# A mixture-of-experts layer on one core: expert slots in 32 places of 256 columns instead of 16 of 512

## The reference

```
x = x + layernorm(attention(layernorm(x)))      # 16 heads, one shared k/v head, causal
x = x + layernorm(moe(layernorm(x)))
moe(x):  probs = softmax(x @ router.T); two best of 8 experts, weights renormalised
         expert e:  silu(x @ gate_e.T) * (x @ up_e.T) @ down_e.T      # 352 inner columns
         plus sigmoid(x @ shared_gate.T) * shared(x)                  # 1408 inner columns
```

## Time and profile before

| | us |
|---|---|
| median of three executions | 2177.38 |
| the profiled execution | 2180.47 |
| its span, first to last instruction | 2178.7 |
| attention | 0 to about 803 |
| routing and the first gathers | 803 to 877 |
| experts, first gate matmul to end of last down | 877.10 to 1424.24 |
| shared expert | 1429.46 to the end |

### The profile page before, as it was taken

The page is one execution under the profiler, slowest core; times in us unless marked ns, Lnnn a source line. Parts: engine busy times, 40 slices in busy tenths (PEclk is TensorE's granted clock), DMA queues, the critical chain, the costliest instruction groups (busy, mean ns, idle before and its releaser), DMA issues. The chain is left out here.

```text
span 2178.7 us, 30973 instructions
## 1 busy us (share of the span) xinstructions
PE 1989.7 (91%) x10858; PEld 1520.2 (70%) x10858; DVE 1037.5 (48%) x2158; ACT 700.6 (32%) x1350; POOL 468.4 (22%) x1045
## 2 busy tenths in 40 slices
PE   4989999999998723999999999999999999999995
PEld 3665656656666413777788888878888788888884
DVE  4556766666665328444445555443432424334243
ACT  3445545454454210344444444332111111111111
POOL 1223424233333221111111111001112021120212
PEclk9799999999998855999999999999999999999998
DMA  5134353343532213344445545332023020230202
GB/s 174 54 106 129 112 181 116 123 143 113 184 108 95 97 77 130 127 156 156 156 143 197 202 145 203 146 122 83 20 97 116 21 97 20 97 116 20 97 20 97
DMA packets 107019, 250.36 MB, mean 115 GB/s; under 512 B 10753, under 2 KB 25345, under 8 KB 99617
## 3 DMA queue, kind: packets, MB, share of 16 engines
q1 hardware_dynamic: 95392, 211.14, 28.4%
q0 software_dynamic: 11520, 37.76, 5.5%
HBM read 165.76 MB, written 79.69 MB: 113 GB/s over the span
## 5 line engine op out<-in xcount | busy, mean ns | idle before, releaser
L1251 PE MATMUL ex_bank<-ex_xT,ex_gu 128*128 128x512 f32 (+14 forms) x1656 | 346.8, 368 | 5.4 <-DVE ex_xT L1285 5.4
L1251 PEld LDWEIGHTS ex_bank<-ex_xT,ex_gu 128*128 128x128 f32 (+1 forms) x1656 | 277.9, 183 | 70.4 <-DVE ex_xT L1285 5.9
L1301 DVE TENSOR_TENSOR sh_silu<-sh_silu,sh_bank 128x512 f32<-128x512 f32 x88 | 60.5, 688 | 459.7 <-ACT sh_silu L1294 453.4
L1251 PE MATMUL sh_bank<-sh_xT,sh_gate 128*128 128x512 f32 x1056 | 256.3, 392 | 7.2 <-DVE sh_dn L1707 5.2
L1263 PE MATMUL sh_bank<-sh_dn,sh_act 128*128 128x512 f32 x1056 | 254.3, 390 | 0.0
L1251 PE MATMUL sh_bank<-sh_xT,sh_up 128*128 128x512 f32 x1056 | 253.6, 389 | 0.0
L671 DVE TENSOR_REDUCE at_nmax<-at_bank 128x1 fp32r<-128x384 f32 (+3 forms) x512 | 222.3, 476 | 61.2 <-PE at_bank L432 60.8
L1294 ACT ACTIVATE sh_silu<-sh_bank 128x512 f32<-128x512 f32 x88 | 52.6, 598 | 593.7 <-PE sh_bank L1251 540.8
L1251 PEld LDWEIGHTS sh_bank<-sh_xT,sh_gate 128*128 128x128 f32 x1056 | 199.6, 189 | 50.0 <-issue 8.4
L1263 PEld LDWEIGHTS sh_bank<-sh_dn,sh_act 128*128 128x128 f32 x1056 | 197.6, 188 | 43.7 <-DVE sh_act L1310 2.9
L1251 PEld LDWEIGHTS sh_bank<-sh_xT,sh_up 128*128 128x128 f32 x1056 | 198.2, 188 | 41.2
(11 more groups left out here) (228 smaller groups left out, 2567.7 us busy)
## 6 DMA issues: line engine op xcount, KB each, us to landing
ex_gu_in<-gu_in SPq DMA_DIRECT2D x23, 1408.0 KB, 9.1
at_Qs<-q_dram SPq DMA_DIRECT2D x96, 256.0 KB, 4.1
ys<-sh_yk SPq DMA_DIRECT2D x17, 1024.0 KB
q_dram<-at_q_h SPq DMA_DIRECT2D x64, 256.0 KB, 3.8
xnT<-at_xT SPq DMA_DIRECT2D x16, 1024.0 KB, 5.0
sh_xT<-xnT SPq DMA_DIRECT2D x16, 1024.0 KB
ex_dn_in<-dn_in SPq DMA_DIRECT2D x23, 512.0 KB, 9.8
at_x_in<-x_in SPq DMA_DIRECT2D x8, 1024.0 KB, 5.3
```

The lines of the kernel that those rows point to most:

```text
L1251: last = self.nc.tensor.matmul(self.gate_up_ps[c % 2][which][0:m, 0:w], cols(i, k), self.xT[j][:, k, 0:w], start=(step == 0), stop=(step = ...
L1301: nc.vector.tensor_tensor(silu[c % 2][0:m, 0:w], silu[c % 2][0:m, 0:w], gate_up_ps[c % 2][1][0:m, 0:w], ALU.mult).then_inc(s["product"], 1)
```

## The change

`TE` = 256 takes the place of `TS` = 512 in the expert stage and in routing (the shared expert keeps 512). Whole places are 32 of 256, rests are 224, 192, 160, 128, 96, 64 and 32 columns: 39 tiles, 9088 columns, 74 blocks. 24 tiles run in the loop, 15 are written out, in the same alternation. A whole tile has two blocks (`QE`), so `down` and its results take two banks, and the two free banks (`x_ps`) take the transposes. `xT` is doubled (one per r). The next tile's rows are transposed behind gate/up 0 (chunks 0, 1) and gate/up 1 (chunks 2, 3) of the present tile, and split at once behind silu and the product; all three `down` come behind gate/up 2. The weights' splits are dealt out as 2, 2, 3 pieces. PE waits for only the four gate/up pieces at the start of a tile, and for the others ahead of `down`. The first rows and weights of the shared expert are loaded in the last two turns of SP.

```diff
-FULL = 2 * NB * S // TS
-PLACE_WIDTH = [TS] * FULL + [TS * (E - 1 - j) // E for j in range(E - 1)]
+TE = 256
+QE = TE // P
+FULL = 2 * NB * S // TE
+PLACE_WIDTH = [TE] * FULL + [TE * (E - 1 - j) // E for j in range(E - 1)]
-LOOPED = 8
+LOOPED = 24
-    TURN = [PIECES[0:3], PIECES[3:5], PIECES[5:7]]
+    TURN = [PIECES[0:2], PIECES[2:4], PIECES[4:7]]
-        xT = [sb(f"xT{j}", [P, C, TS], F32R) for j in range(2)]
+        xT = [[sb(f"xT{r}{j}", [P, C, TE], F32R) for j in range(2)] for r in range(2)]
-        gate_up_ps, out_ps = [bank[0:2], bank[2:4]], bank[4:8]
+        gate_up_ps, out_ps, x_ps = [bank[0:2], bank[2:4]], bank[4:4 + QE], bank[6:8]
+        X_TURN = [(0, 1), (2, 3), ()]
+        def transpose_x(pe, n, c, src, tiles):
+            for t in range(tiles):
+                last = nc.tensor.transpose(x_ps[c % 2][:, t * P:(t + 1) * P], src[:, t, c * P:(c + 1) * P], idf[:])
+            last.then_inc(s["xT_done"], 1)
...
# sync
-                elif n == NT - 1:
-                    for b in range(2):
-                        stage.load_x(sp, b, b)
+                elif n == NT - 2:
+                    stage.load_x(sp, 0, 0)
                     for c in range(2):
                         stage.load_weights(sp, c)
+                else:
+                    stage.load_x(sp, 1, 1)
...
# tensor, one tile
                 pe.wait_ge(s["xT_lo"], C * n + C)
+                pe.wait_ge(weights.lo, WN * n + C)
+                for c in range(NC):
+                    g.gate_up(n, c, gate(c), up(c), width(n))
+                    if not last:
+                        if c == 0 and isinstance(n, int):
+                            pe.wait_ge(gathered[1 - r], 16 * gathers_before(n + 2, 1 - r))
+                        elif c == 0:
+                            pe.wait_ge(gathered[1 - r], 16 * QE * (pair + 1 + r))
+                        for x in X_TURN[c]:
+                            pe.wait_ge(s["xT_lo"], C * n + C + x - 1)
+                            transpose_x(pe, n + 1, x, xg[1 - r], BLOCKS[n + 1] if isinstance(n, int) else QE)
                 pe.wait_ge(weights.lo, WN * n + WN)
                 for c in range(NC):
-                    g.gate_up(n, c, gate(c), up(c), width(n))
...
+                    g.down(n, c, lambda k: weights.dn_s[r][k][0:rows[c], c, :], blocks(n), blocks_before(n))
...
# scalar (vector likewise, with gate_times_up, low_x, split_lo)
                     gate_silu(nc, n, c, rows, silu, gate_up_ps, s, width(n))
                     if not last:
+                        for x in X_TURN[c]:
+                            high_x(n + 1, x, xT[1 - r], ahead)
                         for _ in TURN[c]:
...
-                if not last:
-                    for c in range(C):
-                        high_x(nc, n + 1, c, xT, gate_up_ps, s, ahead)
```

More of the change, by code:

```diff
@@ L53 @@
 SC = PLACE_COLUMN[NT]
-LOOPED = 8
-PLACE_OF = [*range(LOOPED), FULL, 8, FULL + 6, 9, FULL + 5, 10, FULL + 4, 11, FULL + 3, 12, FULL + 2, 13, FULL + 1, 14, 15]
+LOOPED = 24
+PLACE_OF = [*range(LOOPED)]
+for j in range(E - 1):
+    PLACE_OF += [FULL + (E - 1 - j) % (E - 1), LOOPED + j]
+PLACE_OF += [*range(LOOPED + E - 1, FULL)]
 WIDTH = [PLACE_WIDTH[p] for p in PLACE_OF]
@@ L63, in blocks_before @@
 def blocks_before(n):
-    return BLOCKS_BEFORE[n] if isinstance(n, int) else QT * n
+    return BLOCKS_BEFORE[n] if isinstance(n, int) else QE * n
 def width(n):
-    return WIDTH[n] if isinstance(n, int) else TS
+    return WIDTH[n] if isinstance(n, int) else TE
 def blocks(n):
-    return BLOCKS[n] if isinstance(n, int) else QT
+    return BLOCKS[n] if isinstance(n, int) else QE
 PASSES = ((0, 0), (0, 1), (1, 0))
@@ L1163, in _ @@
             steps.then_wait(nc.vector.tensor_copy(whole_i[:, 2, :], n_of))
-            nc.vector.tensor_scalar(whole_i[:, 0, :], whole_i[:, 2, :], TS.bit_length() - 1, None, ALU.logical_shift_right)
-            steps.then_wait(nc.vector.tensor_scalar(whole_i[:, 1, :], whole_i[:, 2, :], TS - 1, None, ALU.bitwise_and))
+            nc.vector.tensor_scalar(whole_i[:, 0, :], whole_i[:, 2, :], TE.bit_length() - 1, None, ALU.logical_shift_right)
+            steps.then_wait(nc.vector.tensor_scalar(whole_i[:, 1, :], whole_i[:, 2, :], TE - 1, None, ALU.bitwise_and))
             nc.vector.tensor_copy(ends[0][:], whole_i[:, 0, :])
@@ L1197, in _ @@
             steps.then_wait(nc.vector.tensor_reduce(shift_rest[:], at_place[:], AX_X, ALU.add))
-            steps.then_wait(nc.vector.tensor_scalar(whole[:, 0, :], whole[:, 0, :], float(TS), None, ALU.mult))
+            steps.then_wait(nc.vector.tensor_scalar(whole[:, 0, :], whole[:, 0, :], float(TE), None, ALU.mult))
             steps.then_wait(nc.vector.tensor_tensor(shift_rest[:], shift_rest[:], whole[:, 0, :], ALU.subtract))
-            steps.then_wait(nc.vector.tensor_scalar(shift_whole[:], first[:], float(TS), None, ALU.mult))
+            steps.then_wait(nc.vector.tensor_scalar(shift_whole[:], first[:], float(TE), None, ALU.mult))
             steps.then_wait(nc.vector.tensor_tensor(shift_rest[:], shift_rest[:], shift_whole[:], ALU.subtract))
@@ L1268, in down @@
             last.then_inc(self.s["down_done"], 1)
[L1270 to L1286, removed]
 def gate_silu(nc, n, c, rows, silu, gate_up_ps, s, w=TS):
@@ L1406, in build_experts @@
         rows, NC, WN, TURN = weights.ROWS, weights.NC, weights.WN, weights.TURN
-        xg = [sb(f"xg{r}", [P, QT, D]) for r in range(2)]
-        index = [sb(f"index{r}", [P, QT], U32) for r in range(2)]
-        xT = [sb(f"xT{j}", [P, C, TS], F32R) for j in range(2)]
-        silu = [sb(f"silu{r}", [P, TS]) for r in range(2)]
-        act_s = [[sb(f"act{r}{j}", [P, TS], F32R) for j in range(2)] for r in range(2)]
+        xg = [sb(f"xg{r}", [P, QE, D]) for r in range(2)]
+        index = [sb(f"index{r}", [P, QE], U32) for r in range(2)]
+        xT = [[sb(f"xT{r}{j}", [P, C, TE], F32R) for j in range(2)] for r in range(2)]
+        silu = [sb(f"silu{r}", [P, TE]) for r in range(2)]
+        act_s = [[sb(f"act{r}{j}", [P, TE], F32R) for j in range(2)] for r in range(2)]
         y_out = stage.yk[1]
         bank = [ctx.enter_context(nc.psum_tensor(f"ex_bank{i}", [P, 512], F32)) for i in range(8)]
-        gate_up_ps, out_ps = [bank[0:2], bank[2:4]], bank[4:8]
+        gate_up_ps, out_ps, x_ps = [bank[0:2], bank[2:4]], bank[4:4 + QE], bank[6:8]
         s = {name: sem(name) for name in GATED_SEMS}
@@ L1417, in build_experts, with high_x, low_x @@
         index_ready = [sem(f"index_ready{r}") for r in range(2)]
+        X_TURN = [(0, 1), (2, 3), ()]
         block = ctx.enter_context(nc.Block())
+        def transpose_x(pe, n, c, src, tiles):
+            for t in range(tiles):
+                last = nc.tensor.transpose(x_ps[c % 2][:, t * P:(t + 1) * P], src[:, t, c * P:(c + 1) * P], idf[:])
+            last.then_inc(s["xT_done"], 1)
+        def high_x(n, c, dst, w):
+            nc.scalar.wait_ge(s["xT_done"], C * n + c + 1)
+            nc.scalar.activation(dst[0][:, c, 0:w], x_ps[c % 2][:, 0:w], ACT.Copy).then_inc(s["xT_hi"], 1)
+        def low_x(n, c, dst, w):
+            nc.vector.wait_ge(s["xT_hi"], C * n + c + 1)
+            nc.vector.tensor_tensor(dst[1][:, c, 0:w], x_ps[c % 2][:, 0:w], dst[0][:, c, 0:w].bitcast(F32),
+                                    ALU.subtract).then_inc(s["xT_lo"], 1)
         def turns(engine, turn):
@@ L1439, in store @@
                 else:
-                    sp.dma_start(ys[:, bass.ds(QT * n, QT), :], y_out[:]).then_inc(stored, 16)
+                    sp.dma_start(ys[:, bass.ds(QE * n, QE), :], y_out[:, 0:QE, :]).then_inc(stored, 16)
             def turn(n, r, pair):
@@ L1457, in gather @@
             def gather(n, r, uses):
-                columns = (bass.ds(QT * n, QT) if not isinstance(n, int) else
+                columns = (bass.ds(QE * n, QE) if not isinstance(n, int) else
                            slice(PLACE_COLUMN[PLACE_OF[n]], PLACE_COLUMN[PLACE_OF[n]] + BLOCKS[n]))
@@ L1482, in _ @@
         def _(pe):
-            g = GatedProducts(nc, pe, rows, xT, act_s, gate_up_ps, out_ps, s)
-            pe.wait_ge(gathered[0], 16 * QT)
+            products = [GatedProducts(nc, pe, rows, xT[r], act_s, gate_up_ps, out_ps, s) for r in range(2)]
+            pe.wait_ge(gathered[0], 16 * QE)
             for c in range(C):
-                g.transpose_x(xg[0], c, idf)
+                if c >= 2:
+                    pe.wait_ge(s["xT_lo"], c - 1)
+                transpose_x(pe, 0, c, xg[0], QE)
             def turn(n, r, pair):
+                g = products[r]
                 def gate(c):
@@ L1493, in up @@
                     return lambda j, k: weights.gu_s[r][j][:, k, I_MOE + c * P:I_MOE + c * P + rows[c]]
-                def down(c):
-                    g.down(n, c, lambda k: weights.dn_s[r][k][0:rows[c], c, :], blocks(n), blocks_before(n))
                 last = n == NT - 1 if isinstance(n, int) else False
                 pe.wait_ge(s["xT_lo"], C * n + C)
```

(18 more changed lines are left out.)

## The result

Four executions of the changed kernel took 2146.3 to 2153.74 us, median 2147.11; four of the kernel before 2172.09 to 2180.34, median 2176.7. The ratio is 0.987, 95% interval 0.9854 to 0.9886: 29.6 us faster. The forecast was 2152, range 2138 to 2170.

A forecast was written before the change was run, and what follows sets the result against it. PE's own work was taken to bound the expert stage: 547.1 to 522.7 us is -24.4, +2.4 for loop waits, -3 at the start, together -25, for a median of 2152 us, range 2138 to 2170.

The forecast's parts named there:

- Whole tiles: Expert stage: a 256-column tile takes 13.5 us on PE, 32 take 432; halving a whole place is worth nothing in itself.
- Rests: Expert stage's remainder tiles: 10.7 us each for 32 to 128 columns, 12.6 each for 160 to 224; the gain is here.
- Clock: Narrow remainder tiles of 32, 64 and 96 columns: 2.6 falls of PE's granted clock at 4.0 us each, 10.5 us.
- Rival 1: Narrow remainder tiles of the expert stage: no fall of the clock, -10.5 us, 2142 us; chance 0.17.
- Rival 2: Clock falls in all three narrow remainder tiles and stays down into the whole tile behind: another +9.5, 2162 us; chance 0.12.
- DVE: Expert stage: DVE's third product starts 10.34 us into a tile, 0.45 us in hand; loop waits cost 2.4 us.
- Rival 3: DVE sets the tile: third product 1 us later, PE stands 0.5 us in 24 to 32 tiles, 2164 us; chance 0.13.
- PE's waits: Expert stage: PE's 5.4 us of waits for the low half of the next tile's rows go.
- DMA: Expert stage: 3.21 MB a tile, 238 GB/s, taken as hidden; a rival has weight loads decide, 2222 us, chance 0.08.
- the start: From the first tile's gathers and routing to the expert stage's first product: -3 us in sum.
- Routing: Ahead of the expert stage: 32 more memsets and ten longer operations cost together +2 us.
- the gathers' landing: First tile: two gathers in place of four, rows land sooner; saves 2.5 to 6 us, 4 taken.

The follow-up runs named there:

- the old dealing: The changed kernel with weight pieces dealt out as before, 3, 2, 2 in place of 2, 2, 3: 2155.86 us, ratio 0.9896 to the kernel before.

## Why the prediction was right, step by step

- *Whole tiles*: 13.5 worked out, 13.58 measured, no wait. That halving a place gives nothing in itself holds: 32 x 13.58 = 434.6 against 16 x 26.73 = 427.7.
- *Rests*: those of 160, 192 and 224 columns took 12.4, 12.6 and 12.9, 37.9 in all (37.8 worked out); 96 and 128 took 10.79 and 11.01 (10.7, with 0.21 and 0.41 of the 0.4 for a wait ahead of the last down).
- *Clock*: 2.6 falls of 4.0 us were 2 falls of 4.3 and 5.9 (15.11 and 16.11 over 10.8, and 0.6 in the tile behind the second): 10.2 us for 10.5. Number and size were each off, and made up for each other. Rival 1 failed: the rest of 32 columns was busy for 15.11 of 15.11 us, at 0.66. The Trainium skill's page "TensorE: Matmul & The Clock Gate" (section "HAM oscillation — how this bites in real kernels") lays a lost clock to idle gaps; this trace, where the clock fell without one, disagrees again. Rival 2 failed: the rest of 96 kept 1.00, and the tile behind the 64 lost 0.6 us.
- *DVE*: its third product was right to 0.01 us; the 2.4 us for waits computed in the loop were nothing (13.58 in the loop, 13.59 outside). Rival 3's condition, a third product 1 us later, did not arise; the old dealing shows how near it is.
- *PE's waits*: of the 5.4 us of the earlier trace rows, 1.49 stand ahead of the stage's first product and became 1.01; the other 3.9, inside the stage, went as worked out.
- *DMA*: hidden, also at 290 GB/s.
- *The mis-sized term* is the start: -6.0 us for -3. Routing +2.0 (+2 worked out) and transposes to product 3.75 for 5.16 (-1.4, -1 worked out) were right; the gathers' landing I put at -4, out of 2.5 to 6, and it was -6.5 (from DVE's cast of the index table to the first transposes 13.96 us before, 7.44 after). Two gathers fewer are 2.5 of it. The other 4.0 is a collision: the weight load of the third tile was issued at 864.8, 0.6 us ahead of the end of the last gather's issue, and with that load held back all four land in 2.8 us. In the changed kernel the load comes 1.8 us behind that end. I had named the load and taken only a part of its price.
- *The total*: the stage came to 525.2 us where the sum had 525.1 (522.7, and 2.4 for waits in the loop). That it is so near is luck in part: the whole tiles took 2.6 more than 432, and the loop waits 2.4 less. The median lies 4.9 us below the forecast, and 3.0 of that is the start; the rest is less than attention scatters by.

The stage by terms: 434.6 + 1.6 (first tile, 15.19) + 37.9 + 21.8 + 2 x 10.8 + 10.2 - 2.5 (fewer transposes) = 525.2, the measured length.

## What to carry to other kernels

Price a tile size by its remainders. Where the matmul has a floor (109 to 111 ns here for anything from 96 to 192 columns, at 128 weight columns), a narrow remainder costs nearly what a wide one does, and it may cost more by the clock: here the rests of 32 and 64 columns lost 10.2 us by it, and computing the narrow ones 128 wide gave 9.7 back. A smaller tile pays only if each other engine's work still ends before PE asks for it: lay out the order of that engine with durations from the old trace and look for the last job before PE's next wait, since moving the rows' split from the end of a tile into its middle, with the buffers and the dealing that go with it, was worth 35 us here.

## What I had not expected of the hardware

- A weight load issued 0.6 us ahead of the end of the last gather's issue held the gathered rows back by some 4 us (they landed 6.5 us behind that end, and 2.8 with the load held). A load issued 1.8 us behind that end, and 0.7 ahead of the landing, did not (2.5 in the changed kernel).
- A fall of the clock can come in the tile behind: with the 64-column rest at 128 columns in the kernel before, the clock was 1.00 in the tile and 0.51 some 3 us into the whole tile that followed, while the next 128-column tile of the same profile, with the same stand of PE behind it, and those in the changed order never showed it. What decides between them stays open.
